# A gated cross-attention block on one core: the first batch's score units with one softmax call for each head, and ten rounded weight pieces moved behind the units

## The reference

```
def _qdq(x):
    s = jnp.maximum(jnp.max(jnp.abs(x), axis=-1, keepdims=True) / 127.0, 1e-08)
    return jnp.clip(jnp.round(x / s), -127.0, 127.0) * s
...
q = _qdq(x) @ _qdq(wq).T + bq
kv = cond @ wkv.T + bkv
...
attn = jax.nn.softmax(jnp.einsum('bnhd,bmhd->bhnm', q, k) * scale, axis=-1)
o = jnp.einsum('bhnm,bmhd->bnhd', attn, v).reshape(B, N, C)
out = _qdq(o) @ _qdq(wp).T + bp
...
wq = w.astype(jnp.float8_e4m3fn).astype(x.dtype)
y = jnp.einsum('bsi,io->bso', x, wq)
return y * scale
...
gate = jax.nn.silu(_quantized_matmul(x, gate_w, gate_scale))
up = _quantized_matmul(x, up_w, up_scale)
return _quantized_matmul(gate * up, down_w, down_scale)
...
x = x + jnp.tanh(g_xattn[0]) * _L0_xattn_ref(_layernorm(x, axis=-1), ctx_2048, ...)
x = x + jnp.tanh(g_ffn[0]) * _L0_ffn_ref(_layernorm(x, axis=-1), ...)
```

## Time and profile before

| what | us |
|---|---|
| median of 3 runs | 926.38 (926.37 to 928.3) |
| profiled execution, its own time | 926.46 |
| span of its trace | 924.7 |
| PE busy in the span | 855.6 (93%), granted clock 0.994 |
| DVE, ACT, POOL busy | 675.5, 554.0, 249.7 |
| first score of unit 0 | 74.2 |
| first value product of the chain (V0) | 205.5 |
| first key product of the next batch (K0) | 243.0 |

### The profile page before, as it was taken

How to read it: one execution, slowest core, us unless ns; L and a number is a source line. 1 busy time by engine, 2 the same in 40 slices (tenths; PEclk the granted TensorE clock), 3 DMA queues, 4 the chain that set the end, 5 groups by cost and what they waited for, 6 DMA issues and landing times.

```text
span 924.7 us, 13556 instructions
## 1 busy us (share of the span) xinstructions
PE 855.6 (93%) x4968; PEld 310.5 (34%) x4976; DVE 675.5 (73%) x1306; ACT 554.0 (60%) x693; POOL 249.7 (27%) x236
## 2 busy tenths in 40 slices
PE   5987888999899999999999999999999989998998
PEld 2421121114443332224433342224433322233444
DVE  6887968938666678986866678986867768778222
ACT  5556777653456649884356648885356679961330
POOL 1145789770017700002006720002002210010230
PEclk9998999999999999999999999999999999999999
DMA  9334253410111133300020133300020024200001
GB/s 331 102 86 132 73 139 98 137 57 1 29 46 35 44 112 101 72 1 2 14 60 24 47 103 101 75 16 1 4 49 1 1 50 110 54 1 23 12 0 46
DMA packets 37250, 55.28 MB, mean 60 GB/s; under 512 B 8960, under 2 KB 15424, under 8 KB 37184
## 3 DMA queue, kind: packets, MB, share of 16 engines
q1 hardware_dynamic: 35264, 48.13, 18.5%
q0 software_dynamic: 1920, 6.29, 2.3%
HBM read 31.21 MB, written 4.19 MB: 38 GB/s over the span
## 4 chain that ended last, share of the span: by engine, by line
PE 65%; DVE 14%; ACT 13%; issue 7%; DMA 1%; ACTq 0%; DVEq 0%
PE ps L1362 33%; ACT r L854 9%; PE ps L1543 8%; PE ps L1506 7%; PE ps L1523 7%; PE ps L1485 4%; DVE acc L1098 4%; PE ps L1551 1%; PE ps L1537 1%; PE ps L1346 1%; DVE kst L1073 1%; DVE am L953 1%; ACT xq L813 1%; ACT r L813 1%; ACT r L762 1%
## 5 line engine op out<-in xcount | busy, mean ns | idle before, releaser
L854 ACT ACTIVATE r<-ps 128x1024 f32<-128x1024 f32 x256 | 251.1, 1022 | 64.5 <-PE ps L1506 62.1
L1506 PE MATMUL ps<-qst,kst 97*128 97x512 f16 x512 | 139.7, 385 | 15.2 <-ACT r L854 12.7
L1073 DVE CUSTOM_DVE_ANT_0 kst<-ps,kst 128x512 f32<-128x512 f32 x192 | 124.5, 685 | 30.3 <-PE ps L1485 28.7
L1523 PE MATMUL ps<-r,vv 128*32 128x512 f32 x1024 | 137.3, 608 | 3.4 <-ACT r L854 3.2
L1098 DVE TENSOR_TENSOR acc<-acc,r 128x1024 f32<-128x1024 f32 x120 | 138.6, 1215 | 0.0
L813 ACT ACTIVATE kst<-ps 128x1024 f32<-128x1024 f32 x96 | 98.1, 1022 | 53.4 <-PE ps L1418 53.1
L1362 PE MATMUL ps<-xs,w_gate 128*128 128x512 f16 x384 | 91.0, 380 | 1.5 <-DVE xs L1279 1.5
L1362 PE MATMUL ps<-xs,w_up 128*128 128x512 f16 x384 | 91.1, 380 | 0.0
L1506 PEld LDWEIGHTS ps<-qst,kst 97*128 97x128 f16 x512 | 37.3, 98 | 155.0 <-ACT r L854 109.7
L911 ACT ACTIVATE qst<-ps,gs_c 128x512 f32<-128x512 f32 x48 | 33.0, 687 | 67.7 <-PE ps L1362 67.7
L1308 DVE SCALAR_TENSOR_TENSOR xq<-ps,us_c,qst 128x512 f32<-128x512 f32 x48 | 36.0, 749 | 50.6 <-PE ps L1362 50.6
(11 more groups left out here) (166 smaller groups left out, 1320.9 us busy)
## 6 DMA issues: line engine op xcount, KB each, us to landing
kst<-k_reg SPq DMA_DIRECT2D x192, 64.0 KB
qst<-q_reg SPq DMA_DIRECT2D x192, 32.0 KB
xs<-in_x SPq DMA_DIRECT2D x4, 1024.0 KB, 5.9
cf<-in_ctxT POOLq DMA_DIRECT2D x16, 256.0 KB, 3.5
xres<-in_x SPq DMA_DIRECT2D x3, 1024.0 KB, 5.3
out<-xres SPq DMA_DIRECT2D x12, 256.0 KB, 2.0
acc<-in_down_w SPq DMA_DIRECT2D x10, 256.0 KB, 2.6
vv<-in_wkvT SPq DMA_DIRECT2D x2, 1024.0 KB, 9.9
```

The source lines that it names most:

```text
L854: nc.scalar.activation(prob[:, s:s + 2, :], ps[:, first_bank:first_bank + 2, :], ACT.Exp, scale=SCALE).then_inc(exp_done, 1)
L1073: ins = nc.vector.tensor_tensor_reduce(kept(b, n)[:, k, :], bank(PAIR + k), kept(b, n)[:, k, :], 1.0, -3.0e38, ALU.add, ALU.max, mx[:, g % ...
L1506: mm = nc.tensor.matmul(bank(first_bank + k), kst[0:97, g % 2, j + k, t * P:(t + 1) * P], qst[0:97, g % 2, j + k, :], start=True, stop=True)
L1523: mm = nc.tensor.matmul(ps[j * DH:(j + 1) * DH, O_BANK, :], vv[:, t, h * DH:(h + 1) * DH], prob[:, p_slot(b, u, j), :], start=(t == 0), st ...
```

## The change

- In units 0 to 21 of the first batch (`SINGLES`) each head has its own score, exponential (128x512) and wait: heads alternate between banks 0 and 1. In units 22 to 31 there are two pairs of score banks, (0, 1) and (2, 3), and both scores of a unit are issued before the values.
- The step list of a unit moves: D and R stand at its end on PE, behind `sums`; S and W stand in its middle (`UNIT_MIDS0`), ahead of `sums`. ACT takes a unit's D one unit later, between head 1 and head 2. The W steps move from units 8 and 10 to 24 and 25, with the scalings of `bp_bc` and `ds_bc` on ACT, which stood ahead of the units.
- Of the 36 weight pieces 6 stand before the units, 20 in them, 10 behind them (`W_LATE`; tiles 8 to 11 and 0 to 5 of down). On DVE the late ones stand behind the quantised output (2), behind the values V1 to V3 (2), behind the normalised x (2), before and after the queries (1 and 1), and beside K3 and K5. POOL rounds four behind its `residual_bias` and six behind the second `inverse_deviation`.
- `WP_UNITS`, `WP_ROWS`, `AHEAD_UNITS`, `W_VARIANCE`, `W_AHEAD`, `W_STACK` and `W_ALL` (28 to 24) take new numbers.

```
-SCORES = ((0,), (0, 6, 2))
+SCORES = ((0, 2), (0, 6, 2))
...
-UNIT_ENDS0 = {PARTS * g - 1 - _first: [("S", g - 1, 0)] for g in range(2, G + 1)}
-UNIT_ENDS0.update({8: [("W", 0, 0)], 10: [("W", 1, 0)]})
+UNIT_MIDS0 = {PARTS * g - _first: [("S", g - 1, 0)] for g in range(2, G + 1)}
+SINGLES = len(DIFFS) - _first
+UNIT_MIDS0.update({SINGLES + 2: [("W", 0, 0)], SINGLES + 3: [("W", 1, 0)]})
...
-WP_UNITS, WP_ROWS = (0, 1, 2, 3, 4, 5, 6), (4, 6)
+W_NONE = (2, 3, 5, 6, 8, 9, 11, 13, 15, 17, 19, 21)
+WP_UNITS, WP_ROWS = (2, 3, 5, 6, 8, 9, 11), (6, 9)
...
-W_AHEAD = {"keys1": 5, "shift0": 8, "queries1": 10, "shift1": 14, "stack2": 16, "shift2": 21, "stack3": 23,
-           "shift3": 29, "residual": 30}
+W_AHEAD = {"keys1": 5, "shift0": 8, "queries1": 10, "shift1": 13, "stack2": 14, "shift2": 17, "stack3": 18,
+           "shift3": 20, "residual": 26}
...
+def single(b, u):
+    return b == 0 and u < SINGLES
...
 def score_bank(b, u, j):
+    if single(b, u):
+        return j % 2
...
         gate_steps("gate", gate_w, w_gate)
-        down_steps(range(DOWN_FREE, FT))
+        down_steps(range(DOWN_FREE, DOWN_FREE + 2))
         gate_steps("up", up_w, w_up)
+        down_steps(range(DOWN_FREE + 2, FT))
         down_steps(range(DOWN_FREE))
...
                 pool.wait_ge(act_setup, 2)
                 residual_bias(0)
+                pool.wait_ge(pe_setup, 3)
+                for k in range(W_STEPS - W_LATE, W_STEPS - W_LATE + W_CHAIN):
+                    round_weights(k)
...
                 inverse_deviation(variance_of_x2(b))
+                if b == 0:
+                    for k in range(W_STEPS - W_LATE + W_CHAIN, W_STEPS):
+                        round_weights(k)
+                    pool.wait_ge(w_done, W_STEPS)
...
-                    for j in range(0, HG, 2):
+                    heads = 1 if single(b, u) else 2
+                    for j in range(0, HG, heads):
+                        if j == 2 and b == 0 and u >= 1:
+                            differences(0, UNIT_STEPS0[u - 1])
...
-                    if b > 0:
-                        scores(b, u, 2)
+                    scores(b, u, 1 if single(b, u) else 2)
                     if u >= 1:
                         values(b, u - 1)
-                    if b == 0:
-                        for s in UNIT_STEPS0[u]:
-                            maxima(b, s)
+                    if single(b, u):
                         scores(b, u, 2)
+                        scores(b, u, 3)
+                    for s in UNIT_MIDS0.get(u, []) if b == 0 else []:
+                        maxima(b, s)
                     if u >= 1:
                         sums(b, u - 1)
+                    for s in UNIT_STEPS0[u] if b == 0 else []:
+                        maxima(b, s)
```

More of the change, by code:

```diff
@@ L1275, in _ @@
                     down_tile(b - 1, 3, b, "LATE3")
+                late_magnitudes(2)
                 next_v(7)
@@ L1504, in scores @@
                         released(b - 1, [n for n in d_seq(b - 1) if d_bank(b - 1, n) == first_bank + k][-1])
-                for k in range(2):
+                for k in range(1 if single(b, u) else 2):
                     mm = nc.tensor.matmul(bank(first_bank + k), kst[0:97, g % 2, j + k, t * P:(t + 1) * P],
```

85 lines of the change are left out of this document (49 added, 36 removed).

## The result

The changed kernel takes 930.61 us (median of 8 executions, 928.05 to 931.93); the kernel before took 926.44 in the same session (8 executions, 926.34 to 928.3). The ratio is 1.0035, 95% interval 1.0021 to 1.0049: slower, by 2 to 4.5 us. The profiled execution took 928.53 with a span of 926.7, 2.0 more than the span of before.

A forecast was written before the change was run, and what follows sets the result against it. It took PE and ACT's alternating waits in the first batch's 4.0 us units as the bound, then DVE behind V0. First stretch -4.4, last ten units -1.8, chain +8.9: +2.7 on 926.46, median 929.0; 8-in-10 range 918 to 936.

The forecast's parts named there:

- The unit: First 22 units: with single heads the period falls from 4.0 to PE's own 3.41, taken as 3.43 us.
- the rival in which single heads do not shrink the unit: First 22 units: ACT over 0.6 a head keeps the unit at 3.8, giving 935 us; chance 0.08.
- wp's rows: After units 6 and 9: ACT's integer rows wait for DVE's quantising, PE stands about 2.4 twice, +4.8 us.
- The row of group 2: Ahead of unit 16: row's DMA issued behind the load of piece 16, so PE waits +4.2 us (0 to 4.7).
- The clock behind it: After the stand ahead of unit 16: about 6.7 us at half clock lose 3.4 us (0 to 3.4).
- The last ten units: Units 22 to 31 up to V0: two pairs of banks, 35.1 against 36.9 us, so -1.8.
- a wait for group 3's row 0.5: Last ten units: PE's wait for this row's DMA, put at 0.5 us within the 35.1.
- Contention of the residual, +1.0: Behind V0: one or two of DVE's four output scalings collide with POOL's additions, +1.0 us (0 to 2.9).
- Pieces 28 and 29: Behind V0: their late loads hold up DVE's V4 and the projection, +5.4 us including 1.0 for slowed scalings.
- Piece 32 and the clock in the chain: Before the queries: late load, +2.0 us; clock may fall as PE stands before X2T, +1.5 (0 to 3).
- the waits are covered: Rival, first batch: SP's row and wp tiles come in time, 12.4 go, 916.7 us; partly, 921 to 924; chance 0.33.
- the clock falls at each stand: Rival, units 7, 10, 16 and X2T: 3.4 us each; two more falls and a half-speed start, 937 us; chance 0.12.

The follow-up runs named there:

- the kernel with the two stands alone: Changed kernel with reordered rows, late pieces moved and GpSimd's pieces earlier (909.43 us), but ACT's integer rows again at units 6 and 9: 914.74, 915.37, 915.55 us.

## Why the prediction came out

It said 929.0, slower than before rather than faster; it was 930.61. Its sum, +2.7 from the first 22 units to the first key product, stands against +2.0 in the trace. The mechanism was right in most terms, but that the sum came so near is in good part luck: up to unit 22 it reckoned 3.0 us more than came, in the last ten units 3.5 less, and behind V0 1.2 more. Its terms, in its own order:

- **The unit.** 3.43 predicted, 3.40 measured. ACT had no part in it, and the rival in which single heads do not shrink the unit falls. Unit 2 came 7.8 after the first score, against 10.75: 3.0 less, predicted 2.8.
- **wp's rows.** Twice 2.4 predicted, 1.88 and 2.04 measured, at the predicted units: 0.9 too much.
- **The row of group 2.** 4.2 predicted, 3.87 measured, for the predicted reason; taking the load from in front of the row took the stand away.
- **The clock behind it.** 3.4 predicted; unit 16 took 4.93 instead of 3.40, so 1.5. The term took the whole 6.7 us of the earlier trace rows at half clock; the stretch was shorter here. This term was mis-sized.
- **Units 2 to 21** in all: 82.0 predicted (69.6 + 4.8 + 4.2 + 3.4), 79.2 measured.
- **The last ten units.** 35.1 predicted, 38.6 measured: the worst miss. A period of 2.82 instead of 3.0 helped by more than one us. But the wait for the row of group 3, put at 0.5, was 2.50, and half clock behind it was not in the sum. The step that failed is "a wait for group 3's row 0.5": it left out DVE's normalisation ahead of the row (2.42) and the two loads ahead of it in the DMA queue (a landing of 3.88, not 2.3; without the loads, but behind twelve stack DMAs, it was 2.96), though the order showed both. "DVE does not gate this" was wrong at this one place.
- **V0.** 6.2 sooner predicted; 4.9 in the trace's own time, 5.8 counted from the first score: the misses above cancel.
- **Contention of the residual, +1.0.** Zero in the changed kernel (1.68), and up to 2.75 on the scalings once POOL's bias began later after V0. The mechanism was right, and its size hangs on how far V0 comes ahead of POOL's last pieces, which a single number could not say.
- **Pieces 28 and 29.** 5.4 with the contention, so 4.4 without; 4.1 measured.
- **Piece 32 and the clock in the chain.** 2.0 and 1.5 predicted. From the projection to K0 passed 22.65, against 19.05 before (its K0 at 242.97, the projection in the earlier trace rows): 3.6, of them 0.82 PE and DVE waiting for the load, the rest the magnitudes and the half clock from 235 to 245. Moving the pieces took all but 1.4 of the 7.7 away, and of these 1.4 the contention has 1.0 (2.42 instead of 1.68, and 0.45 instead of 0.17 for the step ahead of it). This shows the cause; how it splits between load and clock is not settled.

**The rivals.** That the waits are covered falls: all four were there. That the clock falls at each stand held in part, and I gave it too little. In the profiled execution the stands of 2 us left it alone; in three traces of other kernels with the same two stands it fell behind one or both of them. This is the likely source of the 2.1 by which the median lies above the profiled execution: of the eight executions the two shortest (928.05 and 928.53) have granted clocks of 0.987 and 0.989, the two longest (931.66 and 931.93) have 0.982, and in the kernel with the two stands alone the same two put back 6.0, not 4. The Trainium skill (TensorE: Matmul & The Clock Gate, section HAM oscillation) describes a kernel in which each wait for a DMA, longer than the work between two of them, let the clock fall and was paid for once more. The stands of 3.8 to 3.9 ahead of unit 16 agree with it. For the two stands of 2 us, which are shorter than the work between them and so not that case, the prediction reckoned with 6.8 on top of their length; the runs give about 2, some executions paying in units 7 and 10 and some not.

What the prediction did not see at all is that its parts were separable: each stand hung on one or two numbers in a table, and with the order of the late pieces 23 us lay in them.

## What to carry to other kernels

When a unit gets shorter, everything whose place was chosen against its old length is due again: for each wait across queues (a row behind a load, a subtraction behind a quantising, a variance) work out anew when it is made and what stands ahead of it on DVE and on the DMA queue, before judging the shorter unit by the total. An engine off the path that ends late, as GpSimd here, takes part of a gain back by slowing another one down, and moving its work earlier gave that part back. An optional piece may stand behind a wait, but nothing on the path may stand behind it: the late pieces cost 7.7 us in one order and 0.3 in another.
